# Convolution layers: factors spread by 32-row fp32 matmuls into slots of four PSUM banks, one root chain for input and output factors

## What is computed

```python
def _logmap0(y):
    n = jnp.maximum(jnp.linalg.norm(y, axis=1, keepdims=True), EPS)
    return _artanh(sc * n) * y / (sc * n)
def _hconv(x, w, b):
    return _project(_expmap0(_conv3x3(_logmap0(x), w, b)))
out = _hconv(x, w1, b1); out = _hbn(out, g1, beta1); out = _hrelu(out)
out = _hconv(out, w2, b2); out = _hbn(out, g2, beta2); out = _hrelu(out)
x = x + out
```

## Time and profile before

| | us |
|---|---|
| median of 3 runs | 12165.35 |
| lowest and highest | 12158.26, 12189.29 |
| the profiled execution | 12163.17 |
| its span in the trace | 12161.4 |
| PE busy (81% of the span) | 9807.8 |
| DVE busy (81%) | 9817.2 |
| ACT busy (69%) | 8395.9 |

### The profile page before, as it was taken

The page is one execution under the profiler, slowest core; times in us unless marked ns, Lnnn a source line. Parts: engine busy times, 40 slices in busy tenths (PEclk is TensorE's granted clock), DMA queues, the critical chain, the costliest instruction groups (busy, mean ns, idle before and its releaser), DMA issues. The chain is left out here.

```text
span 12161.4 us, 365018 instructions
## 1 busy us (share of the span) xinstructions
PE 9807.8 (81%) x152226; PEld 5058.3 (42%) x152226; DVE 9817.2 (81%) x12823; ACT 8395.9 (69%) x5579; POOL 298.1 (2%) x132
## 2 busy tenths in 40 slices
PE   1899979997665789968888888888888888888788
PEld 0444434443443666633333333333333333333355
DVE  6788857776777666659998989899999889999787
ACT  0454534444552123339999999999999999999688
POOL 0000000000000620000000000000000000000000
PEclk9999989998887999979999999999999999999899
DMA  7777757776663234445555555555555555555466
GB/s 261 211 218 223 215 173 227 222 226 192 269 272 118 72 104 153 152 100 104 105 103 108 101 106 103 105 100 109 100 106 104 105 106 103 106 103 103 130 203 190
DMA packets 1165582, 1796.51 MB, mean 148 GB/s; under 512 B 124832, under 2 KB 929824, under 8 KB 1094048
## 3 DMA queue, kind: packets, MB, share of 16 engines
q1 hardware_dynamic: 1164320, 1777.49, 57.0%
HBM read 701.15 MB, written 402.65 MB: 91 GB/s over the span
## 5 line engine op out<-in xcount | busy, mean ns | idle before, releaser
L1764 DVE SCALAR_TENSOR_TENSOR grown_ex<-ratio,ex 128x2048 f32<-128x2048 f32 x1024 | 2330.5, 2286 | 280.1 <-PE out L1897 101.9
L1897 PE MATMUL out<-ex,kan_basis 32*32 32x512 f32 x32768 | 1502.4, 643 | 635.5 <-DVE z L1746 314.6
L1642 ACT ACTIVATE ex<-ex 128x2048 f32<-128x2048 f32 x1024 | 1925.6, 1898 | 4.1
L1897 PE MATMUL out<-grown_ex,kan_basis 32*32 32x512 f32 x32768 | 1611.6, 641 | 36.4 <-DVE grown_ex L1764 35.3
L459 PE MATMUL conv<-uc,w 128*32 128x512 f32 x12288 | 1377.1, 596 | 48.3 <-DMA uc<-u 47.4
L419 ACT ACTIVATE v<-conv,cb 128x512 f32<-128x512 f32 x512 | 350.7, 685 | 1112.9 <-PE conv L459 1105.4
L1638 ACT ACTIVATE ex<-kin,offset 128x2048 f32<-128x2048 f32 x512 | 1016.2, 1993 | 95.0 <-PE out L1897 82.7
L1897 PEld LDWEIGHTS out<-ex,kan_basis 32*32 32x32 f32 x32768 | 403.8, 106 | 1160.2 <-issue 1092.6
L1897 PEld LDWEIGHTS out<-grown_ex,kan_basis 32*32 32x32 f32 x32768 | 557.5, 106 | 611.1 <-issue 510.5
L459 PEld LDWEIGHTS conv<-uc,w 128*32 128x32 f32 x12288 | 390.9, 109 | 906.3 <-issue 871.5
L2016 DVE TENSOR_TENSOR d<-xt 128x2313 f32<-128x2313 f32 (+2 forms) x256 | 621.0, 2494 | 118.8 <-PE acc L2073 117.8
(11 more groups left out here) (287 smaller groups left out, 18720.1 us busy)
## 6 DMA issues: line engine op xcount, KB each, us to landing
uc<-u SPq DMA_DIRECT2D x2048, 129.0 KB, 2.8
xt<-in_x SPq DMA_DIRECT2D x128, 1024.0 KB, 7.0
t<-v SPq DMA_DIRECT2D x128, 1024.0 KB, 4.4
back_k<-ku SPq DMA_DIRECT2D x1024, 128.0 KB, 5.1
xt<-in_x SPq DMA_DIRECT2D x32, 2048.0 KB, 7.6
xt<-t SPq DMA_DIRECT2D x64, 1024.0 KB, 7.3
tt<-t SPq DMA_DIRECT2D x64, 1024.0 KB, 10.2
x<-x SPq DMA_DIRECT2D x64, 1024.0 KB, 4.6
```

Source lines behind the costliest of these rows:

```text
L1642: a.activation(ex[:, j], ex[:, j], ACT.Exp, scale=-1.0).then_inc(exps, 1)
L1764: v.scalar_tensor_tensor(grown_ex[:, j % 2], ratio[:], LARGEST, ex[:, j], ALU.min, ALU.mult).then_inc(grown, 1)
L1897: last = m.matmul(out[rows(i), g, :], k["kan_basis"][rows(g), kind - 1, n, :], base[rows(g), cols(i)], start=(n == 0), stop=(n == BASES - ...
```

## The change

Only `conv_layer` changes (and the last digits of the constants `RSQRT`, which cost no time). A spread is now one plain fp32 matmul per block with 32 rows of the matrix and of the factor (`tile_position=(QUAD * bank, 0)`); four blocks lie in the array's four row groups and write four different banks. The four banks of `spread` are one slot of 8 blocks, filled five times in a band's round (input: 8, 8 and 4 blocks; output: 8 and 8), and DVE takes a slot by one to three products. The high/low split is gone. Both inverse roots come from one chain of polynomial steps on `[P, 2, COLS]`, the input's for band n-1 and the output's for band n-3. The orders of the work on PE, DVE, ACT and SP are rewritten; `load` also waits for `normed`, since `xn` and `sq` are now made at separate places. Statistics of half 1 are taken a round later.

```diff
+def rsqrt_keeping(dve, y, q, t, a):
+
+    dve.tensor_scalar(y.bitcast(I32), q.bitcast(I32), -0.5, 1597463007.0, ALU.mult, ALU.add)
+    dve.drain()
+    dve.tensor_tensor(t, y, y, ALU.mult)
...
+    dve.drain()
+    dve.scalar_tensor_tensor(y, a, RSQRT[0], y, ALU.add, ALU.mult)
+    dve.drain()
+
...
-        sp1 = sb("sp1", [P, 2, COLS])
-        q2, y2, t2, m2 = (sb(k, [P, COLS]) for k in ("q2", "y2", "t2", "m2"))
-        sp2 = sb("sp2", [P, 2, COLS])
-        pc1 = net.ps(local, "pc1", [P, BANK])[:, 0:COLS]
-        pc2 = net.ps(local, "pc2", [P, BANK])[:, 0:COLS]
-        spread1 = net.ps(local, "spread1", [P, 2, BANK])
-        spread2 = net.ps(local, "spread2", [P, 2, BANK])
+        part = sb("part", [P, HALVES, CHUNKS2 * 6])
+
+        q, rn, t_, a_ = (sb(k, [P, 2, COLS]) for k in ("q", "rn", "t", "a"))
+        nc_, l1, l2, sl, pl, xx, spread_of_u, spread_of_out = (sb(k, [P, COLS]) for k in (
+            "nclip", "l1", "l2", "sl", "pl", "xx", "factor_u", "factor_out"))
+        pc = net.ps(local, "pc", [P, 2, BANK])[:, :, 0:COLS]
+        spread = net.ps(local, "spread", [P, GROUP, BANK])
...
-                wait_both(sp, u_ready, (2 * r + h + 1) * CHUNKS1, conv_ready, (2 * (r - 1) + h + 1) * 4)
+                wait_both(sp, taken_u if h else u_done, 3 * r + 3 if h else r + 1, conv_ready, (2 * (r - 1) + h + 1) * 4)
...
-                sp.wait_ge(out_ready, (2 * r + h + 1) * CHUNKS2)
+                sp.wait_ge(taken_out, 2 * r + h + 1)
...
-            def squares(r, _):
-                for h in range(HALVES):
-                    wait_past(act, summed1, 2 * (r - 1) + h + 1)
...
-                    wait_past(act, u_ready, (2 * (r - 1) + h + 1) * CHUNKS1)
...
-                    a.activation(xn[:, h, :], src, ACT.Identity if first else ACT.Relu, bias=bias_h, scale=scale_h).then_inc(normed, 1)
-                    a.activation(sq[:, h, :], src, ACT.Square, bias=bias_h, scale=scale_h).then_inc(squared, 1)
...
+            def square(r, h):
+                src, scale_h, bias_h = source_of(h)
+                wait_past(act, summed_u, 2 * (r - 1) + h + 1)
+                act.wait_ge(loaded[h], 48 * r + 48)
+                a.activation(sq[:, h, :], src, ACT.Square, bias=bias_h, scale=scale_h).then_inc(squared, 1)
+
+            def normalize(r, h):
+                src, scale_h, bias_h = source_of(h)
+                wait_past(act, taken_u if h else u_done, 3 * r if h else r)
+                act.wait_ge(loaded[h], 48 * r + 48)
+                a.activation(xn[:, h, :], src, ACT.Identity if first else ACT.Relu, bias=bias_h, scale=scale_h).then_inc(normed, 1)
...
-            pipeline_by_two(act, BANDS, [(2, lambda r, parity: evacuate(r, parity, 0, range(4)))] + ([(1, logarithms)] if first else []) +
-                            [(2, lambda r, parity: evacuate(r, parity, 1, (0, 1, 2))), (0, squares),
-                             (2, lambda r, parity: evacuate(r, parity, 1, (3,)))])
+
+            def round_(n, parity):
+                if exists(n - 2):
+                    evacuate(n - 2, parity, 0, (0, 1))
+                if first and exists(n - 1):
+                    logarithms(n - 1)
+                if exists(n - 2):
+                    evacuate(n - 2, parity, 0, (2, 3))
+                if exists(n):
+                    square(n, 0)
+                    square(n, 1)
+                if exists(n - 2):
+                    evacuate(n - 2, parity, 1, (0, 1))
...
+                if exists(n - 2):
+                    evacuate(n - 2, parity, 1, (3,))
+            rounds(act, round_)
...
+                wait_past(pe, read, r)
...
+            def sum_out(r, h):
+                if h == 0:
+                    wait_past(pe, read, r + 2)
+                pe.wait_ge(evacuated, (2 * r + h + 1) * 4)
...
+                last.then_inc(summed_out, 1)
+
+            def spread_blocks(blocks, factor):
+                for b in blocks:
+                    bank, rows = b % GROUP, slice(QUAD * (b % GROUP), QUAD * (b % GROUP) + QUAD)
+                    at = COLS * (b % SLOT // GROUP)
+                    last = m.matmul(spread[:, bank, at:at + COLS], c["sel"][rows, b, :].bitcast(F32), factor[rows, :],
+                                    start=True, stop=True, tile_position=(QUAD * bank, 0))
+                return last
+
+            def fill_u(r, slot):
+                if slot == 0:
+                    pe.wait_ge(factors_u_ready, r + 1)
+                    if not isinstance(r, int) or r >= 2:
+                        pe.wait_ge(taken_out, 2 * (r - 2) + 1)
+                    else:
+                        wait_past(pe, taken_u, 3 * r)
+                else:
+                    pe.wait_ge(taken_u, 3 * r + slot)
+                spread_blocks(range(SLOT * slot, min(SLOT * slot + SLOT, HALVES * HALO)), spread_of_u).then_inc(spread_u, 1)
+
+            def fill_out(r, h):
+                if h == 0:
+                    pe.wait_ge(factors_out_ready, r + 1)
+                    if not isinstance(r, int) or r > 0:
+                        pe.wait_ge(taken_out, 2 * r)
+                    else:
+                        pe.wait_ge(taken_u, 6)
+                elif not isinstance(r, int) or r + 2 < BANDS:
+                    pe.wait_ge(taken_u, 3 * (r + 2) + 3)
+                else:
+                    pe.wait_ge(taken_out, 2 * r + 1)
+                spread_blocks(range(SLOT * h, SLOT * h + SLOT), spread_of_out).then_inc(spread_out, 1)
...
+            def round_(n, _):
+                if exists(n - 2):
+                    convolve(n - 2, 0, (0, 1))
+                if exists(n - 3):
+                    fill_out(n - 3, 0)
+                if exists(n - 2):
+                    convolve(n - 2, 0, (2, 3))
...
-            def norms_u(r, _):
-                dve.wait_ge(summed1, 2 * r + 2)
-                v.tensor_copy(n2[:], pc1).then_inc(read1, 1)
+            def roots(ru, ro):
+                with_u, with_out = exists(ru), exists(ro)
+                both = slice(0 if with_u else 1, 2 if with_out else 1)
+                if with_u:
+                    dve.wait_ge(summed_u, 2 * ru + 2)
+                if with_out:
+                    dve.wait_ge(summed_out, 2 * ro + 2)
+                v.tensor_scalar(q[:, both], pc[:, both], EPS_NORM * EPS_NORM, None, ALU.max).then_inc(read, 1)
                 v.drain()
-                v.tensor_scalar(q[:], n2[:], EPS_NORM * EPS_NORM, None, ALU.max)
-                v.drain()
-                rsqrt_steps(v, rn[:], q[:], t_[:])
...
+                rsqrt_keeping(v, rn[:, both], q[:, both], t_[:, both], a_[:, both])
+                if with_out:
+                    wait_past(dve, spread_out, 2 * ro)
+                    v.tensor_scalar(spread_of_out[:], rn[:, 1], ATANH_MAX, 1.0, ALU.mult, ALU.min).then_inc(factors_out_ready, 1)
+                if with_u and first:
...
-                    v.tensor_tensor(pl[:], pl[:], t_[:], ALU.mult)
+                    v.scalar_tensor_tensor(pl[:], q[:, 0], 0.04, pl[:], ALU.is_lt, ALU.mult)
...
-                v.tensor_scalar(sl[:], sl[:], edge[:, bass.ds(r, 1)], None, ALU.mult)
-                v.drain()
-                wait_past(dve, spread1_ready, 2 * r * CHUNKS1)
-                split_hi_lo(v, sp1[:, 0, :], sp1[:, 1, :], sl[:]).then_inc(factors1, 1)
-
-            def products_out(r, parity, h):
-                for k in range(CHUNKS2):
-                    dve.wait_ge(spread2_ready, (2 * r + h) * CHUNKS2 + k + 1)
-                    cols = slice(BANK * k, BANK * k + BANK)
-                    v.tensor_tensor(v_sb[:, parity, h, cols], v_sb[:, parity, h, cols], spread2[:, k % 2, :],
-                                    ALU.mult).then_inc(out_ready, 1)
-                v.drain()
...
+                wait_past(dve, spread_u, 3 * r)
+                v.tensor_scalar(spread_of_u[:], sl[:], edge[:, bass.ds(r, 1)], None, ALU.mult).then_inc(factors_u_ready, 1)
+
+            def product_u(h, first_row, rows, banks, half):
+                at = slice(COLS * first_row, COLS * (first_row + rows))
+                if half is None:
+                    inside = lambda tile_: tile_.rearrange("p (z k) w -> p z k w", z=2)
+                    factor = spread[:].rearrange("p k (z w) -> p z k w", z=2)
+                else:
+                    inside = lambda tile_: tile_
+                    factor = spread[:, banks, COLS * half:COLS * half + COLS]
...
+            def take_u(r, slot):
+                dve.wait_ge(spread_u, 3 * r + slot + 1)
+                if slot == 0:
+                    wait_past(dve, uc_loaded[0], 256 * r)
+                    dve.wait_ge(normed, 2 * r + 1)
+                    product_u(0, 0, 8, None, None).then_inc(taken_u, 1)
+                elif slot == 1:
+                    product_u(0, 8, 2, slice(0, 2), 0).then_inc(u_done, 1)
+                    wait_past(dve, uc_loaded[1], 256 * r)
+                    dve.wait_ge(normed, 2 * r + 2)
+                    product_u(1, 0, 2, slice(2, 4), 0)
```

(63 more changed lines are left out.)

170 lines of the change are left out of this document (91 added, 79 removed).

## The result

| | us |
|---|---|
| before, median of 4 runs (the three above and one more) | 12171.03 |
| changed kernel, median of 4 runs | 12034.1 |
| lowest and highest | 12020.56, 12046.74 |
| the profiled execution, its span | 12020.56, 12018.7 |

What follows compares the result with a forecast made beforehand. PE was taken to bound the layers' rounds. 30 rounds saving 5.0 and 6.4 us give 342, plus 40 for head and tail, less 15 for full DMA engines: 367 off 12163, about 11795 us, range 11690 to 11895.

Steps and rivals of the forecast that it cites:

- Part 1: Spreads on PE: 14.4 us per round become 5.2, at 1.15 us for a fill of 8 blocks.
- C: Cheaper fills (0.86 us) and overlap, no lag of the loads: 1.2 us less a round, 11725 us; chance 0.15.
- D: Row groups don't run abreast: spreads 16.2 us per round instead of 5.2, about 12480 us; chance 0.03.
- Part 2: Inverse roots on DVE: two chains become one of 6.35 us; DVE's total falls by about 4 us.
- Part 3: Walk through layer 1's round: PE waits of 1.85, 2.45 and 1.7 us; round 41.0 to 36.0, 5.0 us saved.
- Part 5: SP and DMA: same copies and bytes; the DMA engines' share rises to 0.86 in layer 1, 0.94 in layer 2.
- Part 7: Items expected to cost nothing: ACT, statistics moved a round later, other stages.
- Part 4: Walk through layer 2's round: squares cost PE 0.9 us; round 39.7 to 33.3, 6.4 us saved.
- Rival A: DMA engines become the bound in both layers: loads land 2 to 3 us later, 11890 us; chance 0.13.
- rival B: PE's clock falls to 0.96 in the layers: 1.2 us more a round, 11865 us; chance 0.15.

Runs made afterwards that it cites:

- the shifted kernels: Small dummy matmuls ahead of the last stage's TensorE loop: 40 in the changed kernel, 11918.9 us; 24 in the kernel before, 12283.8 us.
- loads_early: Changed kernel plus 40 dummy matmuls before the last loop, each half's loads issued right behind that half's regroup in both layers: 11868.4 us.
- both_phase_0: Changed kernel with loads issued early by halves, 16 dummy matmuls per layer 1 round before the `factor_u` wait, and 8 before the last loop: 11786.9 us.
- no_polynomial: Changed kernel plus 40 dummy matmuls before the last loop, without layer 1's polynomial for small norms on VectorE: 11920.4 us.

## Why the prediction was wrong

**Held.** Part 1: fills at 1.15 us and less, so rivals C and D fall. Part 2: roots from 2311.57 to the fill at 2318.32, 6.75 us with the handover, 6.75 walked. Part 3: the waits of the walk to 0.3 us. Part 5: DMA shares of 0.85 and 0.89 (0.86 and 0.94 forecast, the second for a shorter round). These carry what the two layers saved, 239 us of the 367 forecast.

**Part 7 failed: "At nothing: ... other stages".** This is 101 of the 239 us by which the forecast was off, shown in both directions by the shifted kernels (-108 and +116 us in the stage). Other stages ran the same instructions in the same order, and I took this for the same time. An engine's code also has a place, and the change lengthens it by 1376 instructions. The Trainium skill, Advanced Engine Details and Errata, section ISA Cache, gives TensorE 128 KB in lines of 16 KB, 256 instructions each; the runs agree with pieces of 256 and with a store of about eight, of which seven stay. The trace of before had it, though no row of it was read: 47 waits for issue in the last stage, and 143 instruction packets.

**Part 4 failed by a size.** "lands 7.0 us after issue, at 19": a square waits for all three DMAs of its half, and half 1's were there 9.3 us after the first, at 21.9. I had taken the page's median of one DMA, and layer 1's at that the earlier trace rows; layer 2's own on the same page is 7.3 us. The sum was off too: issued at 8.9 + 3.5 = 12.4, it lands at 19.4 even with 7.0. The sums ended at 25.9 instead of 22.8, 3.1 us in the round shown and 83 us in the layer; with the loads issued early the layer came to 1138.3 us, against 1133.7 forecast, and the rounds to 33.8, against 33.3 walked. Rival A named the symptom (waits for `xt`, sums 2 to 3 us later), and its round of 36 for layer 2 is near the 36.7 measured; its cause, the DMA engines as the bound, is what loads_early refutes.

**Part 3 took the full clock for granted**, and left it to rival B. The waits were right, their after-effect was not in the walk: 1.6 us in the group behind the wait for `factor_u`, in each of layer 1's rounds. Filling the wait gave back 26 of the layer's 45 us; another 17 came back only when the loads were early as well (1206.8 us, against 1205.2 forecast), since behind the slow group stood the same late loads as in layer 2, which part 3 didn't walk. B priced the clock at 1.2 us a round, but in both layers alike. The Trainium skill's rule cited there (TensorE: Matmul & The Clock Gate, The HAM clock gate) says the gate follows how busy the array has lately been; the trace agrees as far as it goes: the clock fell right behind waits, in every round of layer 1 looked at and in three of layer 2. The busy share over a whole round does not tell the layers apart (32.1 of 37.4 and 31.3 of 36.3 us).

The three misses are 45 + 83 + 101 = 229 of the 239 us; the rest is the profiled execution, 14 us below the median, less the 5 us that all else saved, and roundings. both_phase_0, which has all that the forecast took for granted (the clock, loads in time, the last stage near its old place), took 11786.9 us against 11795 forecast, with work added and SP's order changed. The sum's other terms held.

## What to carry to other kernels

When a change adds or removes many instructions, look at every later loop of that engine for idle time "before issue" and for packets on the instruction queue: a loop near or above the instruction store changes its time with its place, and a few dummy instructions ahead of it can be worth almost as much as the change (here 115 us, against 137). Where an operation waits for a set of DMAs, walk with the last one's issue and landing, and with what stands ahead of it in its queue. A wait that is removed shows the next one behind it; two edits that win little singly may win much together.

## What was not expected of the hardware

- TensorE's clock after a wait. In layer 1 of the changed kernel, the group after two waits of 1.65 and 2.24 us that end 8.7 us apart was slow in all 11 rounds looked at. In no_polynomial, of 22 waits of 1.98 to 2.83 us before the second sum of squares, 11 were followed by a slow sum (2.2 us or more instead of 1.49); after the five of 0.27 to 1.85 us none was slow, and after that of 1.97 us the fill behind the sum was (1.24 us instead of 0.71). What tells the slow ones from the others is not known. Filling 1.9 of the 2.24 us with dummy matmuls won 26 us in the layer, and 43 together with the early loads.
- Leaving out one of nine terms, 256 of 2331 instructions in a turn, left the stage at 763 us: the idle time before issue rose from 47.5 to 85.8 us.
- The DMA engines were busy 0.99 to 1.00 of two whole rounds at 264 to 266 GB/s, and hardly held anybody up: from 2150 to 2550 us TensorE waited 1.1 us for `uc` and ScalarE 3.6 us for `xt`.
